# The shared expert's down products moved from ahead of the routed blocks to behind them, in a two-layer attention and mixture-of-experts kernel

## The chip, the core and the metric

The kernel runs on one core of a Trainium2 chip. Times are microseconds of device time for the whole program; the kernel before was run three times, and each run is one number. One further execution was recorded by the hardware profiler; its rows are what the argument rests on. The engines are PE (matrix products), DVE and ACT (elementwise work, with access to the products' accumulators in PSUM), POOL (here it issues indirect DMAs and weight loads) and SP (it issues DMAs only).

## The reference, cut to what matters

Input is 1024 tokens of 384 channels. Layer 0 is dense attention and a mixture of 8 experts; layer 1 is windowed attention and the feed-forward part below, in which the change lies.

```python
B, S, D, F, E, NS = (2, 1024, 384, 768, 8, 1)
def _L1_ffn_ref(x, Wg_s, Wu_s, Wd_s, Wg_r, Wu_r, Wd_r, W_router, expert_bias):
    K_ACTIVE = 2
    ...
    g_s = jax.nn.silu(jnp.einsum('td,edf->etf', xf, Wg_s))
    u_s = jnp.einsum('td,edf->etf', xf, Wu_s)
    shared_out = jnp.einsum('etf,efd->td', g_s * u_s, Wd_s)
    logits = xf @ W_router + expert_bias
    top_vals, top_idx = jax.lax.top_k(logits, K_ACTIVE)
    rw = jax.nn.softmax(top_vals, axis=-1)
    ...
    g_r = jax.nn.silu(jnp.einsum('td,edf->etf', xf, Wg_r))
    u_r = jnp.einsum('td,edf->etf', xf, Wu_r)
    out_e = jnp.einsum('etf,efd->etd', g_r * u_r, Wd_r)
    routed_out = jnp.einsum('etd,te->td', out_e, combine)
    return (shared_out + routed_out).reshape(B, S, D)
```

The caller adds the result to its input, which the kernel holds in `X`. So per token the kernel forms X + shared expert + two weighted rows of routed experts.

## The kernel before, in words

Each engine has its own program, written out by hand; engines meet only at counting semaphores. An instruction that waits holds up everything behind it on its engine. Constants: P = 128 rows to a tile, NT = 8 token tiles, C = 384, ROUTED_BLOCKS = 23, `m.IC` = 6 chunks of the inner width 768, HALF = 2.

Layer 1's feed-forward part runs in this order.

- Routing: DVE finds the two experts of each token and a row for each (token, expert) pair in a list sorted by expert, padded to blocks of 128 rows. POOL scatters the normalised tokens there (`block_rows_in`, 16 indirect DMAs, L858). POOL also loads the shared expert's weights and routed expert 0's (`expert(0, 0)`) early. Two experts' weights fit in SBUF at a time (slots 0 and 1 of `Wgu`, `Wd`). Expert 1 is requested once the shared expert's gate and up products are finished (`shared_psum`), since its slot holds their split weights until then; expert e+2 when the last block of expert e has been copied out (`y_dve`).
- Shared expert, gate and up: PE L1641, 12 groups of 18 products; ACT forms `shared_gate` (L1044) and DVE `shared_hidT` (L1289), in PSUM banks 0 to 5.
- Shared expert, down: PE L1650, eight token tiles of 6 products, each of which runs as two passes, so 96 in the trace. Tile t goes to PSUM bank 3 + t % 3, and DVE adds it to `X` (L1293, semaphore `shared_added`). PE's tile t waits until tile t-3 has been added.
- Routed blocks, 23 of them: PE transposes the block's rows (`transpose_x`, L1662), forms gate and up (`gate_up`, L1676, 18 products), transposes the hidden rows (`transpose_h`, L1685) and forms the down products (`down`, L1697, 12 passes). ACT and DVE copy and combine between (`xbT` L1053, `gated` L1063, `hid` L1309, `hidT` L1071 and L1300), DVE copies the result to `yb` (L1338) and SP stores it to `block_rows_out` (L602). The blocks use banks 0 to 5 in two sets, bank 6 for the transposes and bank 7 for the result. The steps are written so that block b+1's gate and up come before block b's down.
- Final gathers: when the last store has landed, POOL fetches each token tile's two expert rows (`got`, 16 indirect DMAs, L880; four buffers, so tile t waits for tile t-4's last sum), DVE adds them with their weights (L1368, L1370, semaphore `added`), and SP stores the tile to the output (L696).

Of the kernel before, what the change touches and what calls it, by code (L numbers as in the profile page):

```python
# [38 lines left out]
ALU = mybir.AluOpType  # L39
AX = mybir.AxisListType  # L40

P = 128
GRID = 32
T = GRID * GRID
NT = T // P
C = 384
# [6 lines left out]
HALF = T // BANK  # L53
# [44 lines left out]
def build(nc, x, qkv_w, qk_b, v_b, proj_w, proj_b, rel_both, Wr0, br0, Wgu0, bgu0, Wd0, bd0,  # L98
# [17 lines left out]
    with ctx:  # L116
        def sem(name):
            return ctx.enter_context(nc.semaphore(name))


        X = sb("X", [P, NT, C])
# [63 lines left out]
        def at(name, shape, offset, dt=F32):  # L185

            size = 4
            for n in shape[1:]:
                size *= n
            assert arena + offset + size <= nc.sbuf_usable_end, (name, arena + offset + size, nc.sbuf_usable_end)  # L190
            return nc.alloc_sbuf_tensor_at(name, shape, dt, offset=arena + offset)
# [20 lines left out]
        gated = [at("gated0", [P, 2, 768], 73728)]  # L212
        pre = at("pre", [P, 2, 768], 79872)
        hid = [at("hid0", [P, 2, 384], 86016)]
        hidT = [at("hidT0", [P, 2, 3, P], 89088)]
# [10 lines left out]
        I1 = moes[1].I  # L226
# [1 line left out]
        Wd.append(at("Wd1", [P, 2, I1 // P, C], 36864))  # L228
        shared_gu = at("shared_gu", [P, KC, 2 * I1], 55296)
        shared_d = at("shared_d", [P, I1 // P, C], 73728)  # L230
        gated.append(at("gated1", [P, 2, I1], 82944))
        hid.append(at("hid1", [P, 2, I1], 89088))
        hidT.append(at("hidT1", [P, 2, I1 // P, P], 95232))
        shared_hidT = at("shared_hidT", [P, I1 // P, T], 82944)
        shared_gate = at("shared_gate", [P, 2, BANK], 107520)
        xn_hi = at("xn_hi", [P, KC, T], 111616, F32R)
# [14 lines left out]
        PS = ctx.enter_context(nc.psum_tensor("PS", [P, 8, BANK], F32))  # L251
# [81 lines left out]
        shared_hid = sem("shared_hid")  # L333
        shared_y = sem("shared_y")
        shared_added = sem("shared_added")
# [160 lines left out]
        def all_blocks(eng, step):  # L496

            for b in range(FIRST):
                step(b, b % 4, 4)
            with eng.Fori(0, TURNS) as i:  # L500
                for n in range(4):
                    step(i * 4 + (FIRST + n), (FIRST + n) % 4, 4)
            for b in range(LAST, ROUTED_BLOCKS):
                step(b, b % 4, ROUTED_BLOCKS - 1 - b)
# [584 lines left out]
        def _(dve):  # L1089
# [28 lines left out]
            for layer in range(2):  # L1118
# [84 lines left out]
                m = moes[layer]  # L1203
# [21 lines left out]
                for t in range(NT):  # L1225
                    last = dve.max(top8[:, t, :], logits[:, t, :])
                st.wait(last)
                for t in range(NT):
                    last = dve.max_index(top8i[:, t, :], top8[:, t, :], logits[:, t, :])
# [3 lines left out]
                for k in range(TOP):  # L1233
                    last = dve.tensor_tensor(chosen[:, k],
                                             iota_e[:, :].rearrange("p (a e) -> p a e", a=1).broadcast_to([P, NT, E]),
                                             top_f[:, :, k:k + 1].broadcast_to([P, NT, E]), ALU.is_equal)
# [31 lines left out]
                for k in range(TOP):  # L1268
                    last = dve.tensor_tensor(place_k[:, k], place[:, :, :], chosen[:, k], ALU.mult)
# [15 lines left out]
                if layer:  # L1285
                    for n in range(HALF * m.IC):
                        half, f = n // m.IC, n % m.IC
                        dve.wait_ge(shared_silu, n + 1)
                        dve.tensor_tensor(shared_hidT[:, f, half * BANK:(half + 1) * BANK], shared_gate[:, n % 2, :],  # L1289
                                          PS[:, 2 * (n % 3) + 1, :], ALU.mult).then_inc(shared_hid, 1)  # L1290
                    for t in range(NT):
                        dve.wait_ge(shared_y, t + 1)
                        dve.tensor_tensor(X[:, t, :], X[:, t, :], PS[:, 3 + t % 3, 0:C], ALU.add).then_inc(shared_added, 1)  # L1293

                def copy_hT(b, par):

# [64 lines left out]
                for b in range(LAST, m.blocks):  # L1361
                    step(b, b % 4, m.blocks - 1 - b)

                if layer:
                    dve.wait_ge(shared_added, NT)
                for t in range(NT):
                    dve.wait_ge(got_in[t % 4], 64 * layer + 32 * (t // 4 + 1))
                    st.wait(dve.scalar_tensor_tensor(X[:, t, :], got[:, t % 4, 0, :], weight[:, 0, t:t + 1], X[:, t, :],  # L1368
                                                     ALU.mult, ALU.add))
                    dve.scalar_tensor_tensor(X[:, t, :], got[:, t % 4, 1, :], weight[:, 1, t:t + 1], X[:, t, :],  # L1370
                                             ALU.mult, ALU.add).then_inc(added, 1)
                    if layer == 0:

                        statistics(t, added, t + 1)
                        if t % (NT // 2) == NT // 2 - 1:
                            normalise(2, t // (NT // 2), 1e-6)
# [4 lines left out]
        def _(pe):  # L1381
# [55 lines left out]
            for layer in range(2):  # L1437
# [161 lines left out]
                for t in range(NT):  # L1599
# [4 lines left out]
                    for kc in range(KC):  # L1604
                        last = pe.matmul(PS[:, t, 0:C], attT[:, kc, t * P:(t + 1) * P], Wproj[layer][:, kc, :],  # L1605
                                         start=kc == 0, stop=kc == KC - 1)
# [3 lines left out]
                m = moes[layer]  # L1610
# [14 lines left out]
                if layer == 0:  # L1625
                    ranks()
                else:

                    for n in range(HALF * m.IC):
                        half, f = n // m.IC, n % m.IC  # L1630
                        cols = slice(half * BANK, (half + 1) * BANK)
                        pe.wait_ge(xn_lo_ready, KC * (half + 1))
                        pe.wait_ge(gu_lo_ready, f + 1)
                        if n >= 3:
                            pe.wait_ge(shared_hid, n - 2)
                        for up in range(2):
                            hidden = slice(up * m.I + f * P, up * m.I + (f + 1) * P)
                            products = [(w[:, kc, hidden], rows[:, cols]) for kc in range(KC) for w, rows in
                                        ((gu_hi, xn_hi[:, kc]), (gu_hi, xn_lo[kc]), (gu_lo, xn_hi[:, kc]))]
                            for i, (w, rows) in enumerate(products):  # L1640
                                last = pe.matmul(PS[:, 2 * (n % 3) + up, :], w, rows, start=i == 0, stop=i == len(products) - 1)  # L1641
                        last.then_inc(shared_psum, 1)
                        if n == 1:
                            ranks()
                    pe.wait_ge(shared_hid, HALF * m.IC)
                    for t in range(NT):
                        if t >= 3:
                            pe.wait_ge(shared_added, t - 2)
                        for f in range(m.IC):
                            last = pe.matmul(PS[:, 3 + t % 3, 0:C], shared_hidT[:, f, t * P:(t + 1) * P], shared_d[:, f, :],  # L1650
                                             start=f == 0, stop=f == m.IC - 1)
                        last.then_inc(shared_y, 1)
                pe.wait_ge(tables_ready, layer + 1)

                def transpose_x(b, place):
# [57 lines left out]
                gate_up(0, 0, starts)  # L1713
                transpose_x(1, 1)
                if layer:
                    pe.wait_ge(shared_added, NT)
                all_blocks(pe, step)


_OUT = ((1, 32, 32, 384), "float32")  # L1720
# [30 lines left out]
```

## Time and profile before

| | |
|---|---|
| median of three runs | 1172.96 us (1170.58 to 1173.01) |
| the profiled execution's own time | 1172.33 us |
| its span in the trace | 1170.7 us |
| PE matmul busy, share of the span | 1014.7 us, 87% |
| mean granted PE clock | 0.946 of 2.4 GHz |

The span is the profiled stretch from the first to the last instruction; the execution's own time is 1.6 us longer. A PE that is busy is not PE at its peak, since products are pipelined and overlap; what one product costs is better read from the distance between starts. The chain of waits is followed back from the last instruction, at each step to what released it. Line numbers are those of the kernel before; behind the changed places the same lines of the changed kernel are a few numbers lower or higher.

### The profile page before, as it was taken

The page shows a single profiled execution, that of the slowest core. Times are in us where ns is not written, and L with a number is a line of the kernel's source. Part 1 is how long each engine was busy: PE and PEld are TensorE (multiplying, and loading weights), DVE is VectorE, ACT ScalarE, POOL GpSimd, SP SyncE. Part 2 cuts the span into 40 slices and gives each one's busy share as a digit, 9 for nine tenths or more (in the row PEclk, how much of TensorE's full clock was granted, in tenths as well). Part 3 has the DMA queues.
Part 4 walks back from the last instruction along what each step waited for, and adds up shares of the span by engine and source line. Part 5 has one row for each costly group of instructions (what it writes and reads, how often), then busy time and mean ns, then how long its engine had stood idle before and what let it go on. Part 6 is the DMA issues. An engine that isn't in the chain of part 4 may idle for free.

```text
span 1170.7 us, 13655 instructions
## 1 busy us (share of the span) xinstructions
PE 1014.7 (87%) x4561; PEld 589.1 (50%) x4562; DVE 510.8 (44%) x898; ACT 322.1 (28%) x492; POOL 324.8 (28%) x281
## 2 busy tenths in 40 slices
PE   6999999999970999993678899889999999999990
PEld 3755455555430566661356555567554454455550
DVE  4556687788651355552634655731111111111113
ACT  2414554555520122221124554401011111111110
POOL 6515677776726011003210002360001100000005
PEclk9999999999985999997689999989999999999995
DMA  8599217000095157115260200523004434440005
GB/s 285 144 293 273 66 29 152 1 1 1 4 343 210 41 186 257 55 54 152 84 164 2 55 1 18 225 108 129 26 14 159 168 132 148 148 161 27 21 21 168
DMA packets 47114, 132.45 MB, mean 113 GB/s; under 512 B 6865, under 2 KB 25817, under 8 KB 46808
## 3 DMA queue, kind: packets, MB, share of 16 engines
q1 hardware_dynamic: 32424, 67.41, 19.7%
q0 software_dynamic: 14640, 64.36, 15.4%
q8 instruction: 32, 0.52, 0.2%
q14 instruction: 18, 0.15, 0.0%
HBM read 89.88 MB, written 30.87 MB: 103 GB/s over the span
## 4 chain that ended last, share of the span: by engine, by line
PE 71%; DVE 9%; issue 7%; DMA 6%; ACT 4%; POOL 2%; SPq 1%; POOLq 0%; DVEq 0%; ACTq 0%
PE PS L1676 21%; PE PS L1697 10%; PE PS L1472 5%; PE PS L1521 5%; PE PS L1398 5%; PE PS L1641 4%; DMA Wd<-in_Wd_r 4%; PE PS L1502 3%; DVE nmax_part L1156 3%; PE PS L1504 3%; PE PS L1605 3%; PE PS L1650 3%; ACT QB L946 2%; PE PS L1452 2%; DVE exp_acc L1188 2%
## 5 line engine op out<-in xcount | busy, mean ns | idle before, releaser
L1676 PE MATMUL PS<-Wgu,xbT 128*128 x690 | 285.3, 555 | 9.1 <-DMA Wd<-in_Wd_r 5.7
L1676 PEld LDWEIGHTS PS<-Wgu,xbT 128*128 128x128 f32 x690 | 127.9, 191 | 127.3 <-issue 114.4
L962 ACT ACTIVATE expS<-PS 128x1024 f32<-128x1024 f32 (+3 forms) x156 | 135.5, 878 | 135.0 <-PE PS L1504 131.4
L1697 PE MATMUL PS<-Wd,hidT 128*128 x414 | 143.1, 491 | 1.5 <-DVE hidT L1300 0.8
L798 POOL TENSOR_TENSOR exp_acc<-exp_acc,expS 128x512 f32<-128x512 f32 (+1 forms) x65 | 124.5, 1915 | 47.6 <-ACT expS L962 46.7
L1472 PE MATMUL PS<-KS,QA 128*128 128x512 f32 (+2 forms) x288 | 109.9, 429 | 18.6 <-DVE nmax L1156 6.8
L1502 PE MATMUL PS<-QA,KS 128*128 128x512 f32 (+3 forms) x312 | 116.9, 380 | 9.0 <-ACT QB L946 9.0
L1156 DVE TENSOR_REDUCE nmax_part<-PS 128x1 f32<-128x512 f32 x160 | 103.7, 685 | 45.9 <-PE PS L1472 45.1
L1504 PE MATMUL PS<-QB,KS 128*128 128x512 f32 (+3 forms) x312 | 111.5, 363 | 0.0
L1697 PEld LDWEIGHTS PS<-Wd,hidT 128*128 128x128 f32 x414 | 78.7, 191 | 57.6 <-issue 14.3
L1472 PEld LDWEIGHTS PS<-KS,QA 128*128 128x128 f32 x288 | 52.4, 191 | 83.0 <-DVE nmax_part L1156 44.5
L1156 DVE TENSOR_REDUCE nmax<-PS 128x1 f32<-128x384 f32 (+2 forms) x112 | 66.5, 621 | 60.7 <-PE PS L1472 59.4
L1071 ACT ACTIVATE hidT<-PS 128x384 f32<-128x384 f32 x46 | 22.6, 491 | 253.5 <-PE PS L1685 253.5
L880 POOL DMA_INDIRECT got<-block_rows_out,row_i x32 | 31.7, 990 | 209.8 <-DMA block_rows_out<-yb 198.3
L1502 PEld LDWEIGHTS PS<-QA,KS 128*128 128x128 f32 x312 | 59.9, 192 | 39.8 <-ACT QB L946 18.2
L1521 PE MATMUL PS<-expS,V 128*32 128x512 f32 (+3 forms) x624 | 71.6, 531 | 0.1
L826 POOL DMA_DIRECT2D Wgu<-in_Wg_r x8 | 6.0, 756 | 221.9 <-DVE yb L1338 199.7
L1300 DVE COPY hidT<-PS 128x384 f32<-128x384 f32 x23 | 12.8, 558 | 120.4 <-PE PS L1685 120.3
L1504 PEld LDWEIGHTS PS<-QB,KS 128*128 128x128 f32 x312 | 60.1, 193 | 7.3
L1398 PE MATMUL PS<-XnT,Wqkv 128*128 128x512 f32 x120 | 58.2, 645 | 3.4 <-issue 2.0
L1309 DVE TENSOR_TENSOR hid<-gated,PS 128x768 f32<-128x768 f32 x23 | 22.0, 954 | 80.3 <-ACT gated L1063 80.3
L1316 DVE TENSOR_TENSOR pre<-PS,bgu 128x768 f32<-128x768 f32 x23 | 22.0, 958 | 78.2 <-PE PS L1676 70.0
(170 smaller groups left out, 1179.9 us busy)
## 6 DMA issues: line engine op xcount, KB each, us to landing
Wgu<-in_Wgu POOLq DMA_DIRECT2D x8, 1152.0 KB, 6.4
Wgu<-in_Wg_r POOLq DMA_DIRECT2D x8, 1152.0 KB, 6.3
Wgu<-in_Wu_r POOLq DMA_DIRECT2D x8, 1152.0 KB, 8.4
Wd<-in_Wd_r POOLq DMA_DIRECT2D x8, 1152.0 KB, 10.8
xb<-block_rows_in SPq DMA_DIRECT2D x46, 192.0 KB, 2.4
block_rows_out<-yb SPq DMA_DIRECT2D x46, 192.0 KB, 1.8
part_rows<-parts SPq DMA_DIRECT2D x2, 3072.0 KB, 17.3
Wd<-in_Wd POOLq DMA_DIRECT2D x8, 576.0 KB, 7.2
```

Source lines behind the costliest of these rows:

```text
L798: last = pool.tensor_tensor(acc, older, exp_tile(0, c, u)[:, pair, heads], ALU.add)
L962: act.activation(exp_tile(layer, c, unit)[:, pair, :].rearrange("p (b n) -> p b n", b=2)[:, :, lo:hi], PS[:, 2 * pair:2 * pair + 2, lo:hi] ...
L1156: dve.tensor_reduce(dst, src, axis=AX.XY if hb == 0 else AX.X, op=ALU.max, negate=True).then_inc(max_done, 1)
L1398: last = pe.matmul(PS[:, bank, :], Wqkv[layer][:, kc, col:col + P], XnT[:, kc, b * BANK:(b + 1) * BANK], start=kc == 0, stop=kc == KC - 1)
L1472: last = pe.matmul(PS[:, bank + (k - lo) // BANK, 0:n], QA[layer][c % 2][:, g, qt * P:(qt + 1) * P], KS[layer][c % 2][:, g, k:k + n], star ...
L1502: pe.matmul(PS[:, 2 * pair + j, lo:hi], keys, QA[layer][c % 2][:, g, queries], start=True, stop=False)
L1504: last = pe.matmul(PS[:, 2 * pair + j, lo:hi], keys, QB[layer][c % 2][:, g, queries], start=False, stop=True)
L1521: last = pe.matmul(PS[D * g:D * g + D, 6, lo:hi], V[:, kt, vcol:vcol + D], probabilities(c, u, g), start=first, stop=last_one, skip_group_ ...
L1605: last = pe.matmul(PS[:, t, 0:C], attT[:, kc, t * P:(t + 1) * P], Wproj[layer][:, kc, :], start=kc == 0, stop=kc == KC - 1)
L1641: last = pe.matmul(PS[:, 2 * (n % 3) + up, :], w, rows, start=i == 0, stop=i == len(products) - 1)
L1676: last = pe.matmul(PS[:, 3 * par + lo // BANK, 0:n], xbT[:, par, kc, :], Wgu[layer][:, bass.ds(s, 1), kc, lo:lo + n], start=kc == 0, stop= ...
L1697: last = pe.matmul(PS[:, 7, 0:C], hidT[layer][:, par, i, :], Wd[layer][:, bass.ds(s, 1), i, :], start=i == 0, stop=i == m.IC - 1)
```

## The change

Three things, all in layer 1. PE's eight tiles of shared down products stand behind the 23 routed blocks, at the end of PE's program, where before they stood ahead of them; in their old place nothing is left, and the wait for `shared_added` ahead of block 0's step becomes one for `shared_hid`. DVE's eight additions of them to `X` stand in the loop of the final sums, each ahead of its tile's two weighted additions, and each tile's first weighted addition waits for its own tile's `shared_added`. And since `shared_hidT` must now live through the routed blocks, `gated1`, `hid1` and `hidT1`, which shared its place in SBUF, take the place of `shared_gu`, the shared expert's gate and up weights.

```diff
-        gated.append(at("gated1", [P, 2, I1], 82944))
-        hid.append(at("hid1", [P, 2, I1], 89088))
-        hidT.append(at("hidT1", [P, 2, I1 // P, P], 95232))
+        gated.append(at("gated1", [P, 2, I1], 55296))
+        hid.append(at("hid1", [P, 2, I1], 55296 + 4 * 2 * I1))
+        hidT.append(at("hidT1", [P, 2, I1 // P, P], 55296 + 4 * 4 * I1))
...
# DVE, ahead of the routed blocks
-                    for t in range(NT):
-                        dve.wait_ge(shared_y, t + 1)
-                        dve.tensor_tensor(X[:, t, :], X[:, t, :], PS[:, 3 + t % 3, 0:C], ALU.add).then_inc(shared_added, 1)
...
# DVE, the final sums
-                if layer:
-                    dve.wait_ge(shared_added, NT)
                 for t in range(NT):
+                    if layer:
+                        dve.wait_ge(shared_y, t + 1)
+                        dve.tensor_tensor(X[:, t, :], X[:, t, :], PS[:, 3 + t % 3, 0:C], ALU.add).then_inc(shared_added, 1)
+                        dve.wait_ge(shared_added, t + 1)
                     dve.wait_ge(got_in[t % 4], 64 * layer + 32 * (t // 4 + 1))
...
# PE, ahead of the routed blocks
-                    pe.wait_ge(shared_hid, HALF * m.IC)
-                    for t in range(NT):
-                        if t >= 3:
-                            pe.wait_ge(shared_added, t - 2)
-                        for f in range(m.IC):
-                            last = pe.matmul(PS[:, 3 + t % 3, 0:C], shared_hidT[:, f, t * P:(t + 1) * P], shared_d[:, f, :],
-                                             start=f == 0, stop=f == m.IC - 1)
-                        last.then_inc(shared_y, 1)
...
                 transpose_x(1, 1)
                 if layer:
-                    pe.wait_ge(shared_added, NT)
+                    pe.wait_ge(shared_hid, HALF * m.IC)
                 all_blocks(pe, step)
+                if layer:
+                    for t in range(NT):
+                        if t >= 3:
+                            pe.wait_ge(shared_added, t - 2)
+                        for f in range(m.IC):
+                            last = pe.matmul(PS[:, 3 + t % 3, 0:C], shared_hidT[:, f, t * P:(t + 1) * P], shared_d[:, f, :],
+                                             start=f == 0, stop=f == m.IC - 1)
+                        last.then_inc(shared_y, 1)
```

PE's program where the shared gate and up products end and block 0 begins. The names in the rows are the tiles of the text; `xb` holds a block's rows and `ord_i` the blocks' experts. Before:

```order
L1641 MATMUL PS<-xn_hi,gu_lo 128x512
L1650 MATMUL PS<-shared_d,shared_hidT 128x384 x48
L1662 MATMUL PS<-ident,xb 128x128 x3
L1668 TENSOR_LOAD ord_i_95
L1668 ISA x2
```

And of the changed kernel, at the same place:

```order
L1640 MATMUL PS<-xn_hi,gu_lo 128x512
L1653 MATMUL PS<-ident,xb 128x128 x3
L1659 TENSOR_LOAD ord_i_95
L1659 ISA x2
L1662 ISA
```

The row of 48 products is gone from here, and block 0's transposes follow the gate and up products at once. PE's program from the last block's down products to the end of the changed kernel, with the semaphores that its instructions wait for:

```order
L1688 MATMUL PS<-Wd_144,hidT_149 128x384
L1714 MATMUL PS<-shared_d,shared_hidT 128x384 x18
L1714 MATMUL PS<-shared_d,shared_hidT 128x384 [waits shared_added]
L1714 MATMUL PS<-shared_d,shared_hidT 128x384 x5
L116 UNCONDITIONAL_BRANCH
```

Before, the branch followed the last down product; now the 48 products stand between, three tiles without a wait and then five with one each. DVE's program from the last block's copy on, of the changed kernel:

```order
L1335 COPY yb<-PS 128x384 [waits y_stored0,y_psum]
L1364 TENSOR_TENSOR X<-X,PS 128x384 [waits shared_y]
L1367 SCALAR_TENSOR_TENSOR X<-got,weight,X 128x384 [waits got_in0,shared_added]
L1369 SCALAR_TENSOR_TENSOR X<-got,weight,X 128x384 [waits dve_step]
L1364 TENSOR_TENSOR X<-X,PS 128x384 [waits shared_y]
L1367 SCALAR_TENSOR_TENSOR X<-got,weight,X 128x384 [waits got_in1,shared_added]
```

Before, a tile had its two SCALAR_TENSOR_TENSOR here and no more; now each has three instructions, of which the first waits for PE and the second for the gather.

## Rows read from the trace of the kernel before

**Rows 1.** The page: part 1 (busy), and a group of part 5 (idle before, releaser)

```profile
PE 1014.7 (87%) x4561; PEld 589.1 (50%) x4562; DVE 510.8 (44%) x898; ACT 322.1 (28%) x492; POOL 324.8 (28%) x281
...
L1676 PE MATMUL PS<-Wgu,xbT 128*128 x690 | 285.3, 555 | 9.1 <-DMA Wd<-in_Wd_r 5.7
```

**Rows 2.** Stretches of the last 360 us: busy time by engine, clock, DMA

```profile
core 0: us, PE busy (x) PEld busy (x) DVE busy (x) ACT busy (x) POOL busy (x), PEclk, DMA share, GB/s
...
810.00:842.00 32.00, 31.33 (x99) 18.55 (x99) 4.56 (x9) 0.00 (x0) 2.31 (x3) 1.00 0.30 111
1010.00:1141.00 131.00, 130.21 (x405) 68.74 (x405) 21.26 (x31) 16.95 (x30) 2.33 (x3) 1.00 0.16 54
1141.00:1171.00 30.00, 0.20 (x1) 0.00 (x0) 10.53 (x17) 0.00 (x0) 16.10 (x16) 0.55 0.55 164
```

**Rows 3.** The chain that ended last: start us, us, what

```profile
799.97 9.31 PE PS L1641 x41
...
810.67 31.23 PE PS L1650 x96
...
842.26 0.50 ACT xbT L1053
...
843.06 7.99 PE PS L1676 x18
...
865.04 5.15 PE PS L1676 x12
...
1141.24 0.57 DVE yb L1338
1141.83 1.83 DMA block_rows_out<-yb
...
1163.55 3.58 DMA got<-block_rows_out,row_i
1167.16 0.63 DVE X L1368
1167.82 0.62 DVE X L1370
```

**Rows 4.** The timeline at 809 us: start us, us, instruction [idle before]

```profile
809.30 0.60 ACT L1044 ACTIVATE shared_gate<-PS 128x512 f32<-128x512 f32 x1 [3.48 <-PE PS L1641]
809.79 0.19 ACT L1047 ACTIVATE warm<-ones 128x1 f32<-128x1 f32 x1
...
810.67 1.24 PE L1650 MATMUL PS<-shared_d,shared_hidT 128*128 128x384 f32 x3 [1.41 <-DVE shared_hidT L1289]
811.44 0.87 POOL L828 DMA_DIRECT2D Wd<-in_Wd_r  x1
```

**Rows 5.** Line L828, layer 1: an expert's last weights, from issue to landing

```profile
DMA to landing us min/median/max: 6.5/10.3/17.8
```

**Rows 6.** SP's timeline: loads of the first four blocks' rows

```profile
789.29 1.79 SPq L595 DMA_DIRECT2D xb<-block_rows_in  x4
```

**Rows 7.** DVE's timeline: the last two additions of the shared expert

```profile
838.07 0.56 DVE L1293 TENSOR_TENSOR X<-X,PS 128x384 f32<-128x384 f32 x1 [3.32 <-PE PS L1650]
841.94 0.56 DVE L1293 TENSOR_TENSOR X<-X,PS 128x384 f32<-128x384 f32 x1 [3.32 <-PE PS L1650]
```

**Rows 8.** The timeline of the end: gathers and weighted additions

```profile
1143.93 1.00 POOL L880 DMA_INDIRECT got<-block_rows_out,row_i  x1 [116.87 <-DMA block_rows_out<-yb]
...
1148.34 0.62 DVE L1368 SCALAR_TENSOR_TENSOR X<-got,weight,X 128x384 f32<-128x384 f32 x1 [6.54 <-DMA got<-block_rows_out,row_i]
...
1151.55 1.31 POOL L880 DMA_INDIRECT got<-block_rows_out,row_i  x1 [0.30 <-issue]
```

**Rows 9.** PE's timeline at 769 us [idle before]

```profile
769.59 0.77 PE L1641 MATMUL PS<-xn_hi,gu_hi 128*128 128x512 f32 x1 [4.07 <-DVE shared_hidT L1289]
```

**Rows 10.** Two stretches behind it, columns as in the second group

```profile
772.00:774.00 2.00, 2.00 (x7) 1.52 (x6) 0.00 (x0) 0.00 (x0) 1.44 (x2) 0.50 0.40 146
776.00:778.00 2.00, 2.00 (x10) 1.68 (x9) 0.69 (x1) 0.60 (x1) 1.39 (x3) 1.00 0.30 112
```

## The prediction

> **What bounds the kernel now.** I read the page first: PE is busy 87% of the span, and of the other engines none is over 44% [rows 1]. That says PE, but only on average, so I went to the stretches of layer 1's last part. From 1010 to 1141 us PE is busy in 130.2 of 131 us at a granted clock of 1.00; from 1141 to 1171 it is busy in 0.20 of 30 us [rows 2]. So the kernel has two limits there: PE up to the last routed block, and after it a tail in which PE has nothing to do. The chain of waits names what fills the tail: the last block's copy at 1141.24, its store, then POOL's gathers one after another, the last gather's landing, and two DVE additions from 1167.16 [rows 3]. Further up, the same chain runs through PE without a break: gate and up products of the shared expert to 809.3, its down products for 31.23 us from 810.67, then block 0's transposes and, from 843.06, its gate and up [rows 3]. The reader is to see two things: the 31.23 us lie wholly on the path, and 29.5 us of PE (1141.2 to 1170.7) lie idle at the end. Among the routed blocks PE waits for weights four times, 5.7 us in all [rows 1].
>
> **The change, part by part.**
>
> *Taken away ahead of the blocks.* What must be ready when block 0 starts earlier? Its rows: SP issued the four loads at 789.3 [rows 6] and they land long before 809. Its weights were loaded before the shared products. Its copy `xbT` stands on ACT behind the last `shared_gate` (809.30, 0.60 us) and the small `warm` at 809.79 (0.19 us) [rows 4], so it can start at about 809.9; before it started at 842.26 [rows 3]. Shift: 842.26 - 809.9 = 32.3 us. That is more than the 31.23 us of the products, since PE's 1.41 us wait for `shared_hidT` [rows 4] is now passed beside block 0's transposes. The PSUM banks agree: the copy stands behind all the `shared_gate` reads, and block 0's set of banks 0 to 2 is by then read out by DVE. The new wait for `shared_hid` stands behind block 0's gate and up, and is met at about 810.6 by the addition at 809.9; it costs nothing.
>
> *Expert 1's weights.* They were requested at 809.9 and the last piece issued at 811.44 [rows 4], as now, but had until block 2's gate and up at 865.04 to land [rows 3] and now have until 865.0 - 32.3 = 832.7. Landing took 10.3 us in the median and 17.8 at most [rows 5]: 821.7 to 829.2. Covered, by 3.5 us in the worst case; without cover, each us late is a us lost. The later loads are requested by the blocks themselves and move with them: their 5.7 us stay.
>
> *Rehousing.* `gated1`, `hid1` and `hidT1` change their place only. `shared_gu` was read for the last time by the splitting into high and low parts, long before 809. Price nothing; instructions are the same.
>
> *The last block.* Before, its result was there for DVE at 1141.24 [rows 3]. Now at 1141.24 - 32.3 = 1108.9.
>
> *Added behind it, PE.* 96 passes at once: banks 3 to 5 belong to block 21, which is finished, and no tile before the fourth waits. The pace is from the additions: they start 3.87 us apart (838.07, 841.94), each on its tile's end [rows 7]. Eight tiles: 8 x 3.87 = 31.0 us. That pace was held while expert 1's weights came in (DMA share 0.30 over that stretch, clock 1.00 [rows 2]), so I take it beside the gathers too. The bound from below is the same 31.0, from above the same at half clock, 62 (a rival below). The last tile is ready at 1108.9 + 31.0 = 1139.9.
>
> *Added behind it, DVE.* Eight additions of 0.56 us [rows 7] in a loop in which DVE mostly waited. Behind the last tile come one of them and two weighted ones: the rows give 0.66 from one start to the next (1167.16, 1167.82) and 0.62 for the last [rows 3]. So 1139.9 + 0.60 + 0.66 + 0.62 = 1141.8. From the end of the last addition (1168.44) to the end of the span 2.26 us passed before, for the store; the same now: 1144.0.
>
> *The gathers.* Before, the eight tiles' rows were there for DVE from 1148.34 [rows 8] to 1167.16 [rows 3], that is 2.7 us apart. Shifted by 32.3: 1116.0 + 2.7 t. PE's tiles: 1112.8 + 3.87 t. PE's come later from tile 3 on, and at tile 7 by 1139.9 - 1134.9 = 5.0 us. The gathers are not held up by it: POOL begins tile t's at (1143.93 - 32.3) + 2.6 t (16 issues in 19.6 + 1 us, [rows 3, 8]); tile 7's at 1129.8 needs tile 3's sum, which is there at 1124.4 + 1.9 = 1126.3. Nor does PE wait for DVE: tile 4's banks (from 1124.4) need tile 1's addition, which DVE reaches after tile 0's sums, at about 1117.3 + 0.6. So the new tail is PE's: 35.1 us (1108.9 to 1144.0) in place of 29.5.
>
> **The sum**: -32.3 + (35.1 - 29.5) = -26.7 us. Against the profiled execution's own time: 1172.33 - 26.7 = 1145.6. That execution lies 0.6 under the median of the three runs, so for the median 1172.96 - 26.7 = 1146.3.
>
> *Beside POOL's issues.* In the tail DVE gets eight more instructions beside POOL's issues. The nearest row is the gather at 1151.55, which took 1.31 us where the first took 1.00, at a moment when DVE was adding [rows 8]. If each of eight additions held up POOL for its whole 0.56 us, the last gather would land 4.5 us later, at 1139.4, still before PE's last tile: the sum stays. The Trainium skill (SBUF — State Buffer, "Who interferes with whom") says that DVE and GpSimd share a pair of ports and that a DVE instruction with at most one SBUF input, outside the two-port modes, does not contend. By that rule these additions (one input in SBUF, one in PSUM) cost POOL nothing. No row here shows the rule by itself.
>
> **The rivals.**
>
> 1. *Late start of the blocks* (expert 1's weights, or something that the 31 us had hidden). For it: one load of the kind took 17.8 us [rows 5]. Against it: that still lands at 829.2. If PE waited at block 2 for up to 10 us, the end is 1147 to 1156. Chance 0.05.
>
> 2. *The gathers or DVE become the bound of the tail.* It begins where the last gather lands over 5.0 us later than the shift says. For it: the longer gather of [rows 8]. Against it: the 4.5 us above as a worst case. Time 1146.5 to 1150. Chance 0.07.
>
> 3. *PE at half clock behind the blocks: the slower side.* PE waited 4.07 us at 769.59 [rows 9], and in the stretch from 772 the granted clock was 0.50, that is 1.2 GHz; by 776 it was 1.00 again, 2.4 GHz [rows 10]. If the tail's products ran at 1.2 GHz throughout, the eight tiles would take 62 us: 1108.9 + 62 + 4.1 = 1175.0 as span, 31 more than my sum, and 1177.3 for the median, 0.4% slower than before. It decides from 26.7 us of extra on. What would do it is a chain of waits in which PE's tile t waits for DVE's addition t-3, which stands behind the sums of tile t-4, which wait for a gather. Against it: before those products PE has run for over 100 us at 1.00 [rows 2], nothing lies between the last down product and the first shared one, and the waits are met 6 us ahead at tile 4. Chance of the whole 0.02; of a part (one or two tiles at half clock, +3.9 to +7.7: 1150 to 1154) 0.03. The Trainium skill (TensorE: Matmul & The Clock Gate, "What's actually happening") says that the throttled state is the default and activity releases it; rows 9 and 10 agree, in that half clock follows the idle stretch.
>
> 4. *The change frees no path*, because PE must wait at block 0 for what came out of the down products anyway: nothing in the order of instructions shows it, and the time would be that of before within 0.2%. Chance 0.01.
>
> **How the numbers follow.** My own forecast has the rest, 0.82. The likeliest time is 1146.3. Its own range is from the reading of the start (809.9 against 32.3, half a us), the tail (half a us) and the spread of the runs before, which reaches 2.4 us below and 0.05 above their median: 1144 to 1148. Of the rivals only 1 to 3 lie above, with 0.17 together; below lies only the case in which the tail would be the gathers' alone, 1146.3 - 5.6 = 1140.7, and nothing speaks for PE being quicker than 3.87 us a tile. For 8 in 10 I take 1143 to 1150. This kernel's runs tell from no change what is over about 0.2%, or 2.3 us. Faster by more than that: 0.82 + 0.05 + 0.07 + 0.03 = 0.97, which I lower to 0.95 for what I have not thought of; within 0.2%: 0.02; slower: 0.03.
>
> **What the profile of the changed kernel would show.** Right: block 0's gate and up begin at 810.7 and not at 843; the clock stays at 1.00 from there to the end of PE's work; PE's waits for weights stay near 5.7 us; the last `yb` copy at 1108.9; DVE's eight additions of PSUM 3.87 us apart, the last at 1139.9; the chain of waits in the tail runs through PE's shared products and no longer through POOL's gathers; the span is 1144.0. Wrong: a wait of PE at block 2 for `Wd`; a gather in the chain; or additions more than 3.9 us apart. The prediction would be most wrong if PE idled between the tiles of the tail, since it would lose both the wait and the clock.

## The result, and the profile after

The changed kernel took 1143.07 us in the median of four runs (1142.08 to 1145.49), beside 1171.77 us (1168.82 to 1173.01) of the kernel before on the same chip. The ratio is 0.9763, 95% interval 0.9741 to 0.9786: faster by 2.4%. The forecast was 1146.3 from a median of 1172.96, a ratio of 0.9772.

The page of the changed kernel, the same two lines as in [rows 1]; `gate_up` now has line L1667:

```profile
PE 1011.7 (89%) x4561; PEld 587.9 (51%) x4562; DVE 510.3 (45%) x898; ACT 321.9 (28%) x492; POOL 323.9 (28%) x281
...
L1667 PE MATMUL PS<-Wgu,xbT 128*128 x690 | 285.5, 556 | 9.2 <-DMA Wd<-in_Wd_r 5.4
```

PE's busy time is nearly what it was (1011.7 for 1014.7 us), in a span that is 29.1 us shorter (1141.6 from 1170.7). It waits for weights 5.4 us, as before 5.7. Two stretches of the changed kernel, the blocks' last 131 us and what follows, with the columns of [rows 2] (busy by engine, clock, DMA share, GB/s):

```profile
978.00:1109.00 131.00, 130.21 (x408) 69.33 (x407) 21.81 (x32) 16.94 (x30) 2.33 (x3) 1.00 0.15 53
1109.00:1142.00 33.00, 28.35 (x88) 16.34 (x86) 14.12 (x24) 0.00 (x0) 15.26 (x16) 1.00 0.49 143
```

The reader is to see the second row: where PE had been idle beside POOL's gathers it is now busy beside them, at full clock. The chain that ended last, of the changed kernel (start us, us, what):

```profile
807.13 0.60 ACT shared_gate L1044
807.73 0.09 ACT warm L1047
807.82 0.39 ACT xbT L1053
808.21 0.29 issue
808.50 7.99 PE PS L1667 x18
...
1106.39 30.97 PE PS L1714 x96
1137.36 0.02 issue
1137.39 0.56 DVE X L1364
...
1137.98 0.63 DVE X L1367
...
1138.63 0.62 DVE X L1369
```

No gather stands in it any more (in [rows 3] they filled the tail). The 31 us of shared products stand at its end in place of its middle, and block 0's rows are copied on ACT right behind the last `shared_gate`.

To keep apart what the change did and what the run did, I measure two stretches in each trace. The *stage* reaches from the start of ACT's last `shared_gate` to the end of the span, the *tail* from the start of the last `yb` copy on DVE to the end of the span. Before: 1170.7 - 809.30 = 361.4 and 1170.7 - 1141.24 = 29.5 [rows 3, 4]. The changed kernel, DVE's last copy of `yb`:

```profile
1106.43 0.56 DVE L1335 COPY yb<-PS 128x384 f32<-128x384 f32 x1 [4.37 <-PE PS L1688]
```

Stage 1141.6 - 807.13 = 334.5, that is 26.9 less; tail 1141.6 - 1106.43 = 35.2. What remains of the 29.1 us lies ahead of the stage: `shared_gate` came 2.2 us earlier in this trace. Where that comes from is the question of two of the experiments (e1 and e12).

### The profile page after: what moved, and what is told of

Its sections match the earlier page's. It is cut to its first block, busy times and chain, and to the rows that moved or that the text cites. A ratio compares the mean times of both kernels' runs of the same rounds, so it can differ in the third digit from the quotient of the medians.

```text
span 1141.6 us, 13662 instructions
## 1 busy us (share of the span) xinstructions
PE 1011.7 (89%) x4561; PEld 587.9 (51%) x4562; DVE 510.3 (45%) x898; ACT 321.9 (28%) x492; POOL 323.9 (28%) x281
## 4 chain that ended last, share of the span: by engine, by line
PE 71%; DVE 9%; DMA 8%; ACT 5%; issue 4%; POOL 3%; SPq 1%; POOLq 0%; DVEq 0%; ACTq 0%
PE PS L1667 21%; PE PS L1688 10%; PE PS L1471 6%; PE PS L1520 5%; PE PS L1397 5%; PE PS L1640 4%; DMA Wd<-in_Wd_r 4%; PE PS L1501 3%; DVE nmax_part L1156 3%; PE PS L1503 3%; PE PS L1714 3%; ACT QB L946 2%; DMA bd<-in_bd 2%; PE PS L1451 2%; DVE exp_acc L1188 2%
## 5 line engine op out<-in xcount | busy, mean ns | idle before, releaser
L1667 PE MATMUL PS<-Wgu,xbT 128*128 x690 | 285.5, 556 | 9.2 <-DMA Wd<-in_Wd_r 5.4
L1667 PEld LDWEIGHTS PS<-Wgu,xbT 128*128 128x128 f32 x690 | 127.9, 191 | 127.6 <-issue 114.8
```

The costliest lines, as they stand in the source:

```text
L1667: last = pe.matmul(PS[:, 3 * par + lo // BANK, 0:n], xbT[:, par, kc, :], Wgu[layer][:, bass.ds(s, 1), kc, lo:lo + n], start=kc == 0, stop= ...
```

## The experiments

My theory: PE sets every us of the stage and of the new tail; the gain is PE's idle time behind the blocks, filled but for what the three additions and the store need. The rivals: the gathers set the tail; the new places in SBUF give or take something; the clock falls in PE's waits.

The experiments ran on two chips. The kernel before took 1172.64 us in the median on the one of e1 to e4, and 1169.72 (e5 to e8) and 1169.48 (e9 to e12) on the other; ratios are to these, so times of different experiments are better compared by ratio or by stage than by the median. e5, e6, e7, e11 and e12 are one run each, and each stage or tail below is that of one trace.

**e1: only the rehousing.** The kernel before with the three tiles at their new places.

```diff
-        gated.append(at("gated1", [P, 2, I1], 82944))
+        gated.append(at("gated1", [P, 2, I1], 55296))
```

(and `hid1`, `hidT1` behind it).

> The down products stand where they stood before the change; only gated1, hid1 and hidT1 have their new place. My theory (the new places cost and give nothing): the time of the kernel before, within 0.2%; the stretch from the last shared_gate on ACT to the end of the span 361.4 us as in the trace of before. Rival (the new places give the 2 us by which the measured gain is larger than my sum): 2 us less than before, 0.2% faster.

Measured: ratio to the kernel before 1.0001 (0.9986 to 1.0015), over ten runs beside thirteen. Its stage is 1173.1 - 810.22 = 362.9, which is 1.5 more than the 361.4 expected: 0.8 us of it are longer waits for weights (6.4 us in place of 5.7), 0.5 the tail (1173.1 - 1143.08 = 30.0). So the stage of one trace is certain to some 1.5 us only. By the times the rehousing gives nothing; its worth is only that it lets `shared_hidT` live on.

**e2, e3: one tile, or four, ahead of the blocks and the others behind.**

```diff
+                if layer:
+                    pe.wait_ge(shared_hid, HALF * m.IC)
+                    for t in range(k):            # k = 1 in e2, 4 in e3
+                        shared_down(t)
                 pe.wait_ge(tables_ready, layer + 1)
...
                 all_blocks(pe, step)
                 if layer:
-                    for t in range(NT):
+                    for t in range(k, NT):
```

DVE's additions of the first k tiles go with them, and PE waits for these (`shared_added`, k) ahead of block 0's step.

> Tile 0 of the down products ahead of the blocks, the other seven behind. My theory (the new tail is set by PE, 35.2 us long, and the gathers alone would take 29.5): one tile more ahead costs 3.9 us there plus the wait of 1.4 us at the start, and shortens the tail by 3.9, so the time is that of the changed kernel plus 1.2 us (1144.3). Rival (the tail is set by the gathers): plus 5.1 us, 1148.2.

> Tiles 0 to 3 ahead of the blocks, 4 to 7 behind. My theory: ahead 4 x 3.87 + 1.2 = 16.7 us more than the changed kernel, and the tail is now that of the gathers, 29.5 us in place of 35.2: plus 11.0 us, 1154.1. Rival (the gain goes by the count of tiles moved, half of 28.7 for half of the tiles): 1157.4.

Measured: e2 1146.4 us, ratio 0.9784 (0.9756 to 0.9811), stage 1145.5 - 808.07 = 337.4; e3 1157.71 us, ratio 0.9884 (0.9852 to 0.9916), stage 1156.0 - 808.33 = 347.7. Against the changed kernel's stage that is +2.9 and +13.2, where my theory had +1.2 and +11.0 and the rivals +5.1 and (by medians) +14.3. The sums are not mine: they lack some 2 us each, and a plain count of tiles (an eighth and a half of 26.9, that is 3.4 and 13.5) meets them better. By the times alone the rival of e3 stands. The traces, taken apart, say where the us are, and they are not where a count of tiles would put them. At the start both did what was worked out: block 0's gate and up began 6.7 us (e2) and 18.3 us (e3) behind the last `shared_gate`, in place of 1.4. The tail of e3 was 29.2 us, that of the gathers alone, as expected. What its trace has over the sum is in the blocks: PE's first wait for weights was longer (2.38 us, where the first trace of the changed kernel has 1.03), and it ran at half clock behind it. PE's timeline and two stretches of e3:

```profile
876.13 6.91 PE L1683 MATMUL PS<-Wgu,xbT 128*128 x12 [2.38 <-DMA Wd<-in_Wd_r]
...
890.32 5.31 PE L1683 MATMUL PS<-Wgu,xbT 128*128 x12
```

```profile
876.00:878.00 2.00, 1.86 (x3) 0.84 (x4) 0.00 (x0) 0.00 (x0) 0.00 (x0) 0.50 0.37 112
...
880.00:882.00 2.00, 2.00 (x6) 0.83 (x5) 0.00 (x0) 0.00 (x0) 0.00 (x0) 1.00 0.00 0
```

The same twelve passes took 6.91 and 5.31 us (5.41 behind a wait at full clock). All four runs of e3 lie above my 1154.1, so this one trace may not tell the whole of it. The missing 1.9 us of e2 are in the tail, on DVE. DVE's timeline of e2:

```profile
1131.19 0.62 DVE L1373 SCALAR_TENSOR_TENSOR X<-got,weight,X 128x384 f32<-128x384 f32 x1
...
1137.76 0.55 DVE L1367 TENSOR_TENSOR X<-X,PS 128x384 f32<-128x384 f32 x1 [5.95 <-remote]
...
1141.31 0.55 DVE L1367 TENSOR_TENSOR X<-X,PS 128x384 f32<-128x384 f32 x1
```

PE ran its tiles without a gap to 1139.4, and tile 5 was ready at 1112.3 + 5 x 3.87 = 1131.7. DVE stood still to 1137.76 all the same and had not worked off its backlog when PE's last tile was ready: the last addition came 1.9 us late. "Remote" means that the profile finds no instruction that released it. This was in nobody's list; it is taken up below.

**e4: the last additions.** The weighted sums ahead of the addition of the shared product, which then is all that stands behind PE. PE's tile t now waits for `added`, the last of tile t-3's three instructions, in place of `shared_added`.

```diff
-                    dve.scalar_tensor_tensor(X[:, t, :], got[:, t % 4, 1, :], weight[:, 1, t:t + 1], X[:, t, :],
-                                             ALU.mult, ALU.add).then_inc(added, 1)
+                    last = dve.scalar_tensor_tensor(X[:, t, :], got[:, t % 4, 1, :], weight[:, 1, t:t + 1], X[:, t, :],
+                                                    ALU.mult, ALU.add)
+                    if layer:
+                        st.wait(last)
+                        dve.wait_ge(shared_y, t + 1)
+                        last = dve.tensor_tensor(X[:, t, :], X[:, t, :], PS[:, 3 + t % 3, 0:C], ALU.add)
+                    last.then_inc(added, 1)
```

> In the final sums the two weighted additions of a tile stand ahead of the addition of its shared product, so that behind PE's last tile only one of the three is left. My theory (PE's last tile sets the end): the last two additions of 0.66 and 0.62 us leave the path, the end comes 1.3 us earlier, tail 33.9 us in place of 35.2, time 1141.8; a difference of 0.1% that only the trace can show. Rival (gathers or the output stores set the end): no change of the tail.

Measured: 1143.25 us, ratio 0.9766 (0.9732 to 0.98), so nothing that the runs can tell. In the trace the tail is 1141.7 - 1107.82 = 33.9 us, to the tenth what was expected, and the stage 333.4, 1.1 less. PE's last tile sets the end in this trace.

**e5: one PSUM bank.** `PS[:, 3 + t % 3, 0:C]` becomes `PS[:, 3, 0:C]`, and PE waits for `shared_added` at every tile from the second on.

> All eight tiles of the down products behind the blocks go to one PSUM bank, so that PE's tile t waits for DVE's addition of tile t-1, not of tile t-3. My theory (PE sets the tail, and each wait of PE shows at the end): tile 2 waits about 2 us behind the first gather's sums, the others about 0.8 us each; the tail is some 7 us longer, 42 us in place of 35.2, the clock stays at 1.00 since no wait reaches 4 us. Rival (the gathers set the tail, PE's waits are hidden): no change of the tail.

Measured: one run of 1153.18 us, tail 1151.6 - 1109.39 = 42.2 us. PE's timeline:

```profile
1119.33 4.14 PE L1714 MATMUL PS<-shared_d,shared_hidT 128*128 128x384 f32 x12 [1.31 <-DVE X L1364]
...
1124.11 4.14 PE L1714 MATMUL PS<-shared_d,shared_hidT 128*128 128x384 f32 x12 [0.65 <-DVE X L1364]
```

Tile 2 came 5.46 us behind tile 1, the later ones follow one another by 4.78 us and not 3.87, and all of it shows at the end: 42 us had been expected. A tail that the gathers set would have hidden it. The reason that the expectation gives for the clock, that no wait reaches 4 us, does not hold: e3, e7 and e9 have the clock low behind shorter ones.

**e6, e11: PE waits ahead of the tail,** for the last block's store in e6, for the first tile's gathered rows in e11.

```diff
                 if layer:
+                    pe.wait_ge(got_in[0], 64 + 32)      # e11; in e6 y_stored[0] and y_stored[1]
                     for t in range(NT):
```

> PE waits behind the last block, ahead of the shared down products, until the last block's store has landed, about 3.9 us. Theory A (the wait shows at the end, the clock stays): tail 4 us longer, 39.2. Theory B (as at 769 us in the trace of before, where PE waited 4.07 us and ran the next 5.6 us at half clock, which lost 2.6 us more): tail 6.7 us longer, 41.9, and a granted clock of 0.5 for some 5 us at its start.

> PE waits behind the last block until the first token tile's gathered rows have landed, about 7 to 8.5 us. Theory A (only the wait shows): tail 35.2 us plus the wait, 42 to 44. Theory B (the clock falls in the wait and stays at half for some 5.6 us of work, as at 769 us in the trace of before, which lost 2.6 us): 2.6 us more than the wait, 45 to 46.5, and a stretch at 0.50.

Measured: e6 1145.46 us, tail 1143.9 - 1105.94 = 38.0; e11 1154.26 us, tail 1152.7 - 1108.31 = 44.4. PE's rows of the two, and two stretches of e11:

```profile
1108.40 31.23 PE L1716 MATMUL PS<-shared_d,shared_hidT 128*128 128x384 f32 x96 [2.51 <-DMA block_rows_out<-yb]
```

```profile
1115.34 33.13 PE L1715 MATMUL PS<-shared_d,shared_hidT 128*128 128x384 f32 x96 [7.07 <-DMA got<-block_rows_out,row_i]
```

```profile
1112.00:1116.00 4.00, 0.66 (x1) 0.50 (x2) 0.00 (x0) 0.00 (x0) 2.89 (x3) 0.55 0.53 142
1116.00:1120.00 4.00, 4.00 (x9) 2.14 (x8) 0.00 (x0) 0.00 (x0) 2.99 (x4) 0.60 0.56 157
1120.00:1124.00 4.00, 4.00 (x14) 2.39 (x13) 1.79 (x3) 0.00 (x0) 1.25 (x2) 1.00 0.34 98
```

In e6 the store landed sooner than I had reckoned; PE waited 2.5 us, the clock stayed, and the tail grew by 2.8: the wait and no more. That is theory A for this wait, but e3 had the clock low behind 2.38 us, so it says nothing of the next one. e11 has a longer wait: the clock stood at 0.55 and 0.60 in the two stretches around the start of the tail's products at 1115.34, the 96 passes took 33.1 us in place of 31.1, and the tail grew by 9.2, of which 7.1 are the wait. That is the mechanism of theory B, with 2.0 us where I had taken 2.6 from 769 us; the tail of 44.4 lies between the two ranges.

**e7: the gathers 8 us later.** Eight fills of `xn_hi`, which nothing reads any more, ahead of POOL's gathers.

```diff
+                if layer:
+                    for _ in range(8):
+                        st.wait(pool.memset(xn_hi[:, 0, :].bitcast(F32), 0.0))
```

> POOL does eight fills of 128x1024 (0.95 us each, into a tile that nothing reads any more) ahead of the final gathers, so that these start 8 us later. My theory (the gathers have 5 us to spare beside PE's tail): tail 3 us longer, 38.3; PE waits once, about 3 us at tile 4, for an addition that stands behind tile 0's sums. Rival (the gathers set the tail): 8 us longer, 43.2.

Measured: 1148.08 us, tail 1146.5 - 1106.90 = 39.6 us: 4.4 more, where my theory had 3 and the rival 8. Rows of POOL and PE, and a stretch:

```profile
1110.33 8.02 POOL L877 MEMSET xn_hi<- 128x1024 f32 x8 [117.62 <-DMA block_rows_out<-yb]
...
1124.84 17.44 PE L1717 MATMUL PS<-shared_d,shared_hidT 128*128 128x384 f32 x48 [2.50 <-DVE X L1367]
```

```profile
1126.00:1128.00 2.00, 2.00 (x5) 1.06 (x4) 1.28 (x3) 0.00 (x0) 1.46 (x2) 0.50 0.74 236
```

PE waited at tile 4, for the addition behind tile 0's sums, 2.5 us. Then the clock was at 0.50 for a while, and 48 passes took 17.4 us and not 15.5. The first gather stood 7.6 us further behind the last `yb` copy than in the first trace of the changed kernel (11.72 us in place of 4.15), and PE's wait took 2.5 of them. So the additions that PE's tile 4 needs have some 5 us to spare, and when that is used up PE pays twice here, with a wait and with the clock. This is the mechanism of the third rival of the prediction, here on purpose.

**e8 to e10: a better version?** PE's last idle moments in the stage are 0.8 us in the last block, ahead of its down products, and 1.1 us ahead of block 0's gate and up. e8 puts tile 0 into the first, with e4's order of additions; e9 the same, but only the last tile is added late; e10 puts tile 0 into the second, and adds the last tile late; its PE waits for DVE's addition of tile 0 ahead of block 0's step.

```diff
# e8, e9: PE, in the last block's step
+                    if layer and more == 0:
+                        shared_down(0)
                     down(b, par)
# e10: PE, at block 0
                 transpose_x(0, 0)
+                if layer:
+                    pe.wait_ge(shared_hid, HALF * m.IC - 1)
+                    shared_down(0)
                 gate_up(0, 0, starts)
```

> The late addition, and tile 0 of the down products moved into the last block, between its transposes and its down products, where PE waits 0.8 us for a copy. My theory: the last block's result comes 3.1 us later, the gathers have that to spare, PE ends 0.8 us earlier; from the last shared_gate to the end of the span 332.4 us in place of 334.5, 2.1 us less than the changed kernel (1.3 from the addition, 0.8 from the wait). Rival (the gathers become the bound): 0 to 1 us less.

> As e8, but only the last tile's shared product is added behind its weighted sums, the other tiles' ahead of them as in the changed kernel, so that PE's tile 3 no longer waits for an addition that stands behind a gather. My theory (e8 lost its gain to that 1.25 us wait): from the last shared_gate to the end of the span 332.4 us, 2.1 less than the changed kernel's 334.5; PE idles nowhere behind the last block. Rival (the gathers, 3 us later, are the bound): 333.5 or more.

> The last tile's late addition, and tile 0 of the down products ahead of block 0's gate and up, where PE waits 1.08 us for the copy of block 0's rows. My theory: blocks and gathers come 2.8 us later, PE ends 1.1 us earlier, the late addition gives 1.3: 332.1 us from the last shared_gate to the end of the span. Rival (as e2, where one tile ahead cost 5.3 us at the start): 336 or more.

Measured: e8 1141.11 us, ratio 0.9758 (0.9737 to 0.9778), stage 1140.5 - 806.51 = 334.0; e9 1143.8 us, 0.976 (0.973 to 0.9791), stage 1142.2 - 804.22 = 338.0; e10 1142.5 us, 0.9759 (0.973 to 0.9788), stage 1138.3 - 803.56 = 334.7. None can be told from the changed kernel's 0.9763, and no stage came to the 332.1 to 332.4 that I had worked out. The stages of e8 and e9 are those that their rivals gave. The traces show what came in between. In e8 PE's tile 3 waited 1.25 us, since tile 0's bank was free only behind tile 0's gather. In e9 and e10 DVE stood still again, for 5.94 and 5.3 us, and its backlog set the end, 3.0 and 2.3 us later than PE's last tile by itself would have. e9's weights also came later (6.6 us of waits in place of 5.4), and behind one of these waits, of 1.91 us, PE ran at half clock (0.53 from 974 to 976 us), which cost 1.7 us more. DVE's timeline of e9, and PE's:

```profile
1134.46 0.56 DVE L1365 TENSOR_TENSOR X<-X,PS 128x384 f32<-128x384 f32 x1 [5.94 <-remote]
```

```profile
973.31 7.11 PE L1681 MATMUL PS<-Wgu,xbT 128*128 x12 [1.91 <-DMA Wd<-in_Wd_r]
```

The 1.1 us at block 0 did go: in e10 the gate and up began with no wait behind tile 0, at 807.56.

**e12: the changed kernel again.**

> The changed kernel once more, for a second trace. My theory (the stretch from the last shared_gate to the end is fixed by the program, what lies ahead of it varies from run to run): 334.5 us again for that stretch within 0.5, and the last shared_gate anywhere from 806.5 to 810. Rival (the changed program is 2 us quicker upstream of the change too): the last shared_gate at 807.1 again within 0.3.

Measured: 1145.07 us; the last `shared_gate` at 809.01, where the first trace of the same program had it at 807.13; stage 1143.5 - 809.01 = 334.5, equal to the tenth (up to the last `yb` copy, the seven traces that share the program so far have 299.3 to 299.9 us); tail 1143.5 - 1108.35 = 35.2. Over the thirteen traces other than this one the last `shared_gate` lies anywhere from 803.6 (e10) to 810.2 (e1), with programs that are alike up to there. One part of it can be seen: at 70 us of the span, in the first attention, the granted clock was 0.50 in the trace of before and 1.00 in the first one of the changed kernel:

```profile
70.00:72.00 2.00, 2.00 (x4) 1.05 (x4) 1.45 (x2) 0.00 (x0) 0.00 (x0) 0.50 1.03 166
```

```profile
70.00:72.00 2.00, 2.00 (x9) 1.39 (x8) 1.49 (x3) 0.49 (x1) 0.99 (x1) 1.00 1.03 160
```

The first is of the kernel before, the second of the changed one; the clock is the third number from the right. In e12, the changed kernel, it was 0.52 there. So the same program gives 1.9 of the 2.2 us back from one trace to the next, and the rival's 807.1 did not come again. A smaller gain upstream is not excluded: the two traces of the old order (809.3 and 810.2, e1) lie above eleven of the twelve others, and two are too few to tell. DVE's timeline of e12 has the still stand too, in the same program that had none in its first trace:

```profile
1127.12 0.95 POOL L880 DMA_INDIRECT got<-block_rows_out,row_i  x1 [0.30 <-issue]
...
1130.87 0.94 POOL L880 DMA_INDIRECT got<-block_rows_out,row_i  x1 [0.30 <-issue]
1133.79 0.55 DVE L1364 TENSOR_TENSOR X<-X,PS 128x384 f32<-128x384 f32 x1 [7.26 <-remote]
...
1139.31 0.55 DVE L1364 TENSOR_TENSOR X<-X,PS 128x384 f32<-128x384 f32 x1
```

Here it had just been worked off when PE's last tile was ready (1139.31), and cost nothing.

## Why the prediction was right

*The start.* Forecast: the blocks begin 32.3 us earlier, since the 31.2 us of products and most of PE's 1.4 us wait go. Measured within the stage: `yb`'s last copy came 331.9 us behind the last `shared_gate` before (1141.24 - 809.30) and 299.3 after, 32.6 less; the waits for weights have 0.3 of it. ACT's copy of block 0's rows stood right behind `warm`, at 807.82, and block 0's gate and up began 1.4 us behind the last `shared_gate` (808.50 - 807.13), as forecast. The clock was 1.00 in every stretch of 2 us from there to the end of PE's work.

*Expert 1's weights.* No wait of PE at block 2. The four waits for weights are the old ones, 5.4 us for 5.7.

*The rehousing.* Price nothing, as e1 shows with an interval of 0.15% to both sides.

*The tail.* Forecast 35.1, measured 35.2 in both traces. PE's tiles stand 3.87 us apart beside the gathers as they did beside expert 1's weights: 96 passes in 31.0 us. POOL's issues did not grow longer beside the eight new additions: in the first trace of the changed kernel 14 of the 16 took 0.94 or 0.95 us and the first two 1.00. The Trainium skill (SBUF — State Buffer, "Who interferes with whom") says that a DVE instruction with at most one SBUF input, outside the two-port modes, does not contend with GpSimd; these rows agree. They are no test of it, since the weighted additions, with two inputs in SBUF, stood beside issues of 0.95 us too, and single issues of up to 1.34 us occur in other traces (e7) as one of 1.31 did before [rows 8]; what makes those longer is not shown. That PE and not the gathers sets the tail is shown by e5 (its waits come out in full), e4 (additions behind PE's last tile taken away come out in full) and e7 (gathers 8 us later cost 4.4).

*The margin of the gathers.* Forecast 5.0 us at tile 7. It came out smaller in the first trace, since the last store took longer: POOL's first gather began 4.15 us behind the last `yb` copy (1110.58 - 1106.43), where it had been 2.69 before (1143.93 - 1141.24) and was 3.65 in e12. The last gather was issued at 1129.47; with the 3.58 us of [rows 3] it landed at about 1133.1 by estimate, 4.3 us ahead of PE's last tile. The other margin, that of PE's wait at tile 4, was forecast at 6 us and is 5.1: tile 1's addition ended at 1116.74, PE's tile 4 began at about 1121.9. This is the one that e7 measures, where PE waited 2.5 us. Its expectation had 3; the 1.9 more by the clock I had priced only as a rival of the prediction.

*A sign that did not come out.* The prediction would have DVE's eight additions 3.87 us apart and names more than 3.9 as a sign of being wrong. DVE's timeline of the changed kernel:

```profile
1110.30 0.56 DVE L1364 TENSOR_TENSOR X<-X,PS 128x384 f32<-128x384 f32 x1 [3.31 <-PE PS L1714]
1110.58 1.00 POOL L880 DMA_INDIRECT got<-block_rows_out,row_i  x1 [118.34 <-DMA block_rows_out<-yb]
...
1114.98 0.62 DVE L1367 SCALAR_TENSOR_TENSOR X<-got,weight,X 128x384 f32<-128x384 f32 x1 [4.12 <-DMA got<-block_rows_out,row_i]
...
1116.20 0.54 DVE L1364 TENSOR_TENSOR X<-X,PS 128x384 f32<-128x384 f32 x1
```

The first two stand 5.9 us apart, the next follow by 2.6, 3.2 and 3.8, and only the last by 3.87. The sign was badly chosen, not the mechanism: tile 1's addition stands behind tile 0's sums, which wait for a gather, as the prediction itself says where it works out PE's wait at tile 4. What counts is that PE's 96 passes have no gap.

*The sum.* -26.7 forecast, -26.9 in the stage. The medians moved by 28.7 us, from 1171.77, and the ratio's interval holds 0.9772. The 3.2 us by which the measured median lies under 1146.3 are for 1.2 the median of before, which lies that much lower with its fourth run, and for the rest mostly what lies ahead of the stage, which differs from run to run by as much (e12). The time is right by less than the mechanism: 1143.07 lies only 0.07 us inside the stated 1143 to 1150, and two of the four runs lie below it (1142.08 and 1142.97). That it fell inside is in part luck. The range allowed for the spread of the runs before, but hardly for what lies ahead of the stage; the term that the argument is about, -26.7, was met within 0.2.

*What I had not on my list* is DVE's still stand. It is a rival of the second kind (DVE as the bound of the tail), and where it occurred in the changed program it ended just in time. In e2, e9 and e10 it cost 1.9 to 3 us.

## What to carry to other kernels

Look for the stretch in which the bounding engine is idle because another one ends the program, and ask which of its work has no reader before the end. The gain is the work, or the idle stretch less what the other engines must still do behind the last piece, whichever is smaller. Here it was the second: 29.5 - 4.1 = 25.4 us, and 1.3 more because PE's old wait at the start went too. Work it out from two lines, when the last gather lands and when the last product ends. Once such work is in place, shaving the seams is worth little: the 0.8 and 1.1 us sought in e8 to e10 went into waits that appeared elsewhere. And an in-order engine between two others (DVE here, which frees PSUM for PE but waits for gathers) ties them together: the order of its instructions decides how far they may drift apart.

## What the runs showed of the hardware that I had not expected

- *The clock falls behind shorter waits than the 4.07 us of [rows 9], but not each time.* Behind 2.38 us of waiting (e3) and 2.50 us (e7) the granted clock was at 0.50, which is 1.2 GHz, and cost 1.5 and 1.9 us; behind 2.51 us (e6) it stayed at 1.00, 2.4 GHz. Behind 7.07 us (e11) it was low and cost 2.0. Behind 5.66 us, at the last tile of e3, twelve passes took 6.50 us in place of 4.0. And behind 1.91 us (e9) it was low too, twelve passes taking 7.11 us, where behind 2.30 us in e1 the same passes took 5.41. So behind five of these seven waits PE lost another 1.5 to 2.5 us. The Trainium skill (TensorE: Matmul & The Clock Gate, "What's actually happening") has the throttled state as the default that activity releases; these rows agree in that the clock is low behind waits and comes back with the work (0.55, 0.60, 1.00 in e11), and they show that two waits of equal length can come out differently.
- *DVE stands still for 4 to 7 us in the tail without a releaser in the trace,* in e2 (5.95), e4 (3.75), e9 (5.94) and e12 (7.26, of which PE's tile was unfinished for the first 1.2), and in e10 (5.3, put down to PE, whose tile had been ready for 5.2), and not in the first trace of the very program of e12. It was always at the addition of tile 4 or 5, that is at nearly the same place in DVE's program, and it ended 2.4 to 3.6 us after POOL had issued its last gather (e12: 1130.87 and 1133.79; e2: 1134.19 and 1137.76; e10: 1128.21 and 1130.58), about when that gather had landed: in e12 the share of the DMA engines goes from 0.72 (1130 to 1132 us) over 0.43 to 0.00, in e9 from 0.67 to 0.01 behind 1134. So the stand ended with the gathers' traffic. A transfer for DVE's own program, queued behind the gathers, would look like this, but it is a guess: the last transfer of instructions that the trace of e12 records starts at 1109.48, and no experiment settled it. It stays open.
